# A sum over five columns moved from VectorE to additions on GpSimd, with columns outermost in the picture, and the next group's features placed between slices of the patch convolution

## The chip, the cores and the metric

The kernel runs on one NeuronCore of a Trainium2 chip. The metric is device time in microseconds (us) of one execution. Five engines work side by side, each on its own in-order queue, and meet only at semaphores: TensorE (PE: matmuls, PEld: its weight loads), VectorE (DVE), ScalarE (ACT), GpSimd (POOL) and SyncE (SP), which here only issues DMA transfers.

## The reference, cut to what matters

Four residual layers follow each other on 32 images of 32 channels and 32x32 pixels; `_gn` normalises every channel of every image:

```python
x = x + _L0_conv_ref(_gn(x), ...)   # 8x8 patches, each routed to 1 of 8 experts' 3x3 convolution
x = x + _L1_conv_ref(_gn(x), ...)   # one mixed 3x3 convolution per image
x = x + _L2_conv_ref(_gn(x), ...)   # nearest of 512 codes for each pixel
x = x + _L3_conv_ref(_gn(x), ...)   # deformable 3x3 convolution
```

The change touches two of them. The fourth samples each image, for every output pixel and each of 9 taps, at a fractional position:

```python
off = einsum('nchw,oc->nohw', inputs, w_grid) + b_grid
px, py = (base + koff + off + 1) * 0.5 * (W - 1)
sampled = tap(x0, y0, wx0*wy0) + tap(x1, y0, wx1*wy0) + tap(x0, y1, wx0*wy1) + tap(x1, y1, wx1*wy1)
out = conv(sampled, w_conv, strides=(3, 3))
```

The first takes a 10x10 window around each of 25 patches per image, routes by the window's mean (`feat = patched.mean(axis=(2, 3))`, the features) and convolves each patch with the chosen expert's weights.

## The kernel before, in words

The images go through in 8 groups of 4 (4 images x 32 channels fill the 128 partitions). A group g has a **front** (layers one to three, and the offsets of the fourth) and then 32 **tiles** (the sampling of the fourth layer; one tile is 128 output pixels of one image). The tiles of group g-1 are laid between the pieces of the front of group g. Every engine's program calls the same function `front(g)`, which calls `at(slots)` at fixed places: `ROW_SLOTS = {0: (-7, -6), 1: (-6, -4), 2: (-4, -3), 3: (-3, -1), 4: (-1, 0)}` after each of the five slices of the patch convolution, then `Y_SLOTS = (0, 3)`, `POOL_SLOTS = (3, 5)`, `MIX_SLOTS = (5, 7)`, `CONV1_SLOTS = (7, 9)`, `NORM2_SLOTS = (9, 11)`, seven `SCORE_SLOTS`, and so on to `REST_SLOTS`. The numbers count tiles from the group's first. So the order is written out by hand, and is the same on all engines. Behind the last front come 39 tiles with nothing between them (the tail): the last 7 of group 6 and the 32 of group 7.

**A tile** goes like this. SP fetches the tile's row positions, broadcast to all partitions, into one of `SPREADS = 4` buffers `zs` (L308). ACT makes tent weights from them, two activations L514 and one L517, into one of three buffers `tent`, two tiles ahead of PE. PE multiplies tents with the picture into three PSUM banks in turn, one bank for each third of the nine taps (L1014, 12 matmul records a third, 36 a tile): for each output pixel that is three taps x 32 channels x 5 neighbouring columns. DVE multiplies each third by the five column weights `near` (L708, 480 elements) and sums the five columns (L713, a reduction 480 -> 96) into `samp`. PE transposes the 288 sums (L1001), ACT copies them out (L504), and for every fourth tile PE convolves (L990).

PE's order within slot N is: third 0 of tile N, then the transposes L1001 of tile **N-1**, then thirds 1 and 2 of tile N. A third needs its bank read by DVE three thirds ago (`strip_read`).

```python
            def slot(N):
                strips(N, 0)
                if N > 0:
                    turn_samples(N - 1)
                strips(N, 1)
                strips(N, 2)
```

**SP** issues row N+SPREADS+1 of `zs` in slot N, after the wait that frees its buffer. In `NORM3_SLOTS` (slots 21 and 22) it does this for the last time before a long series: `load_slice(k, 1)` and `load_slice(k, 2)`, 12 window transfers (L369) and one of weights (L371) each, and `load_picture`, 16 transfers (L319). Only then does it go on with `zs`, and after slot 25 there is one more `load_slice`, after slot 27 another.

**Features.** DVE normalises the next group's input (L645 to L665), sums the windows (L738, L742) and scales (L746) in one piece after the fifth slice (`features`), before the tiles of `Y_SLOTS`. It copies the windows out (L751, five copies) in the piece that routes the next group and mixes the second layer's weights (after `POOL_SLOTS`). GpSimd only issues the gathers of the experts' weights (L476), 16 in all, and no arithmetic.

Names of stretches used below: the *features piece*, the *pooled piece* (adding the first layer's result, normalising, up to L836, for which PE waits), the *mix piece* (route, windows, mix, up to L785), the *scores* (L1115 on PE, L882 and L884 on DVE: 32 of each per group, one tile between each four).

## Time and profile before

| | |
|---|---|
| median of 3 runs | 2766.87 us (2762.34 to 2772.3) |
| the profiled execution | 2759.06 us |
| its span | 2757.2 us |
| PE busy | 2132.4 us (77%) |
| DVE busy | 1811.6 us (66%) |
| ACT busy | 1524.7 us (55%) |
| POOL busy | 24.7 us (1%) |
| mean granted TensorE clock | 0.911 |
| L708, DVE multiply | 503.6 us, 768 times |
| L713, DVE sum over the columns | 501.5 us, 768 times |

The span is from the first instruction to the last. The shares are averages over stretches with quite different limits: in the tail PE is never idle, within a front it stops for several us at a time. The granted clock is 1.0 at the higher of TensorE's two levels (2.4 GHz).

### The profile page before, as it was taken

How to read it: one execution, taken by the hardware profiler on the slowest of the kernel's cores; microseconds unless marked ns; L12 is line 12 of the kernel's file. 1: busy time of each engine (PE TensorE's matmuls, PEld its weight loads, DVE VectorE, ACT ScalarE, POOL GpSimd, SP SyncE). 2: the span in 40 equal slices, each digit the busy share in tenths (PEclk: the TensorE clock that was granted, in tenths of full speed). 3: DMA queues.
4: the chain of work that ended last, by engine and by line, in shares of the span. 5: the costliest groups of instructions: out<-in, count | busy, mean ns of one | idle time of the engine just before them, and what ended most of it. 6: DMA issues, size and time to landing. Idle time of an engine off the chain costs nothing.

```text
span 2757.2 us, 51316 instructions
## 1 busy us (share of the span) xinstructions
PE 2132.4 (77%) x20658; PEld 1792.4 (65%) x20658; DVE 1811.6 (66%) x3534; ACT 1524.7 (55%) x1803; POOL 24.7 (1%) x35
## 2 busy tenths in 40 slices
PE   0274488787886978878788778878788798887999
PEld 0223465687666966578666776568766696667998
DVE  3365458667686666866677665866758665776776
ACT  0021356466564655556565465646656465656987
POOL 1000000000000000000000000000000000000000
PEclk9686699899998989989999889989899899998999
DMA  6643533273351842436333453327434182113331
GB/s 171 126 132 72 141 106 120 76 161 113 100 147 43 202 123 78 125 92 181 103 105 104 111 155 106 116 79 161 119 98 148 44 199 92 52 48 90 108 116 56
DMA packets 290577, 311.50 MB, mean 113 GB/s; under 512 B 238148, under 2 KB 249092, under 8 KB 286116
## 3 DMA queue, kind: packets, MB, share of 16 engines
q1 hardware_dynamic: 285828, 273.74, 36.5%
q0 software_dynamic: 3360, 30.27, 4.1%
q10 hardware_dynamic: 1152, 4.19, 0.5%
q8 instruction: 165, 2.70, 0.4%
q14 instruction: 72, 0.59, 0.1%
HBM read 251.65 MB, written 56.48 MB: 112 GB/s over the span
## 4 chain that ended last, share of the span: by engine, by line
PE 53%; DVE 19%; DVEq 8%; SPq 7%; ACT 5%; DMA 4%; issue 4%; ACTq 0%; POOL 0%; POOLq 0%
PE bank L1014 37%; PE bank L1096 5%; SPq L369 4%; DVE code L884 4%; DVEq L883 4%; PE bank L1001 3%; DVE samp L713 3%; PE bank L1115 2%; SPq L319 2%; DVE strip L708 2%; PE bank L1074 1%; DVEq L712 1%; ACT diag L581 1%; PE bank L1132 1%; PE bank L1156 1%
## 5 line engine op out<-in xcount | busy, mean ns | idle before, releaser
L1014 PE MATMUL bank<-picture,tent 128*128 128x160 f32 x9216 | 1420.5, 313 | 79.1 <-DVE strip L708 52.2
L1014 PEld LDWEIGHTS bank<-picture,tent 128*128 128x128 f32 x9216 | 1351.5, 201 | 109.5 <-issue 83.2
L708 DVE TENSOR_TENSOR strip<-bank,near 128x480 f32<-128x480 f32 x768 | 503.6, 656 | 586.2 <-PE bank L1014 585.3
L514 ACT ACTIVATE tent<-zs,row_at_sb 128x1152 f32<-128x1152 f32 x512 | 614.5, 1249 | 50.5 <-DMA zs<-z_rows 50.3
L517 ACT ACTIVATE tent<-tent 128x2304 f32<-128x2304 f32 x256 | 543.8, 2124 | 18.8 <-issue 1.7
L713 DVE TENSOR_REDUCE samp<-strip 128x96 f32<-128x480 f32 x768 | 501.5, 653 | 72.4 <-issue 2.7
L504 ACT COPY samp_t<-bank 96x384 f32<-96x384 f32 x256 | 120.6, 471 | 461.9 <-PE bank L1001 461.8
L1115 PE MATMUL bank<-cb,xs 128*128 128x512 f32 x512 | 267.3, 624 | 118.6 <-DVE code L884 86.4
L1115 PEld LDWEIGHTS bank<-cb,xs 128*128 128x128 f32 x512 | 83.3, 191 | 259.4 <-issue 173.7
L574 ACT COPY xs<-xn 32x128 f32<-32x128 f32 x256 | 75.0, 293 | 195.6 <-PE bank L1115 177.8
L1001 PE MATMUL bank<-ident_sb,samp 128*96 128x128 f32 x768 | 138.5, 292 | 53.3 <-ACT fin L500 47.4
L882 DVE MAX8 top<-bank 128x8 f32<-128x512 f32 x256 | 174.7, 682 | 6.2 <-PE bank L1115 6.0
L884 DVE FIND_INDEX8 code<-top,bank 128x8 uint32<-128x512 f32 x256 | 176.8, 691 | 0.3 <-issue 0.3
L493 ACT ACTIVATE sd<-ve 128x1 f32<-128x1 f32 x32 | 6.5, 203 | 247.2 <-DVE ve L654 247.2
L1096 PE MATMUL bank<-xp,bd 128*128 128x512 f32 x288 | 130.9, 603 | 8.6 <-DVE bd L858 8.6
L1001 PEld LDWEIGHTS bank<-ident_sb,samp 128*96 128x96 f32 x768 | 87.8, 134 | 76.2 <-issue 53.9
L581 ACT ACTIVATE diag<-ident_h,code_f 128x128 f16<-128x128 f16 x256 | 81.8, 390 | 74.7 <-DVE code_f L908 74.7
L808 DVE TENSOR_TENSOR yc<-bank,gb 128x320 f32<-128x320 f32 x40 | 19.3, 483 | 124.3 <-PE bank L1074 124.3
L1096 PEld LDWEIGHTS bank<-xp,bd 128*128 128x128 f32 x288 | 53.4, 192 | 68.9 <-issue 60.3
L1074 PE MATMUL bank<-slice 96*32 96x64 f32 x1920 | 36.1, 242 | 71.0 <-DMA slice<-picked_weights 70.4
L1132 PEld LDWEIGHTS bank<-onehot,codes_b 128*32 128x32 bf16 x3072 | 48.5, 103 | 58.4 <-issue 33.1
L1074 PEld LDWEIGHTS bank<-slice 96*32 96x32 f32 x1920 | 34.3, 125 | 73.8 <-DMA slice<-picked_weights 72.9
(125 smaller groups left out, 1061.5 us busy)
## 6 DMA issues: line engine op xcount, KB each, us to landing
zs<-z_rows SPq DMA_DIRECT2D x256, 576.0 KB, 4.2
picked_weights<-arena SPq DMA_DIRECT2D x15, 1800.0 KB
arena<-picked_weights SPq DMA_DIRECT2D x24, 720.0 KB, 6.6
arena<-windows SPq DMA_DIRECT2D x288, 50.0 KB, 4.0
slice<-picked_weights SPq DMA_DIRECT2D x16, 720.0 KB, 6.1
windows<-arena SPq DMA_DIRECT2D x32, 312.5 KB, 5.0
slice<-windows SPq DMA_DIRECT2D x192, 50.0 KB, 2.9
y_patches<-yc SPq DMA_DIRECT2D x32, 160.0 KB, 4.4
```

The lines of the kernel that those rows point to most:

```text
L369: sp.dma_start(xs0[s][C * dy:C * (dy + 1), i], a[:, :, dy * WIN:dy * WIN + CUT]).then_inc(sliced[s], 16)
L504: act.copy(samp_t[:, N % SET], PT[0:PARTK, 0:384].rearrange("p (r n) -> p r n", r=3)).then_inc(samp_sb, 1)
L514: act.activation(w[:, c], zs[:, N % SPREADS, :], ACT.Abs, bias=row_at[:, c:c + 1])
L517: act.activation(w, w, ACT.Relu, bias=1.0, scale=-1.0).then_inc(tent_ready, 1)
L708: dve.tensor_tensor(y, STRIPS[j % 3][:, 0:DENSE * XW * C].rearrange("p (d c x) -> p d c x", d=DENSE, c=C), w.broadcast_to([128, DENSE, C, ...
L713: m = dve.tensor_reduce(samp[:, N % 2, PARTK * d:PARTK * (d + 1)], strip[:, j % 2], AX.X, ALU.add)
L882: dve.max(top[:, i, :], SCORES[n % 2][:, :])
L884: dve.max_index(code[:, i, :], top[:, i, :], SCORES[n % 2][:, :]).then_inc(score_read, 1)
L1001: m = pe.transpose(PT[0:PARTK, 128 * r:128 * (r + 1)], samp[:, N % 2, PARTK * r:PARTK * (r + 1)], ident[:])
L1014: m = pe.matmul(STRIPS[j % 3][:, XW * C * e:XW * C * (e + 1)], tent[:, N % TENTS, c, DENSE * d + e], picture[:, b % 2, i, c], start=(c == ...
L1096: m = pe.matmul(PP[1 + h][:, :], bd1[:, d, :], grid1[:, y:y + H // 2, d % 3:d % 3 + W], start=(d == 0), stop=(d == TAPS - 1))
L1115: pe.matmul(SCORES[n % 2][:, :], xs2[:, i, :], cb2[:], start=True, stop=True).then_inc(score_done, 1)
```

## The change

1. **The sum goes to GpSimd.** The picture is kept with columns outside channels (ACT's copy L525 now copies straight), so that the product strip is laid out tap, column, channel. DVE only multiplies. The reduction over five columns becomes three GpSimd additions per third: columns 0,1 += columns 2,3 (192 elements), column 0 += column 4 (96), samp = column 0 + column 1 (96), with a drain between them. PE's transposes wait for these (`added`). DVE may be three thirds ahead (`STRIPPED = 3`).
2. **SPREADS is 3** instead of 4.
3. **The next group's features** are split: normalising after slice 2, window sums after slice 3. The windows are copied out after the first tile of `Y_SLOTS`. SP sends the means out before the y transfers and fetches them after.
4. **Gathers.** Both halves of the picked weights have a place in the arena; GpSimd issues both gathers one after the other, between the additions of tiles 10 and 11 of a group. `q2` gets a buffer of its own.

```diff
-SPREADS = 4
+SPREADS = 3
+STRIPPED = 3
-                act.copy(picture[:, b % 2, i].rearrange("p k (c x) -> p k c x", c=C),
-                         raw[:, i].rearrange("p k (x c) -> p k c x", c=C)).then_inc(picture_ready, 1)
+                act.copy(picture[:, b % 2, i], raw[:, i]).then_inc(picture_ready, 1)
...
+            def tiles(first, end):
+                for N in range(max(first, 0), end):
+                    for d in range(THIRDS):
+                        j = THIRDS * N + d
+                        pool.wait_ge(strip_read, j + 1)
+                        if d == 0 and N >= 2:
+                            pool.wait_ge(samp_turned, N - 1)
+                        y = strip[:, j % STRIPPED]
+                        pool.tensor_tensor(y[:, :, 0:2], y[:, :, 0:2], y[:, :, 2:4], ALU.add)
+                        pool.drain()
+                        pool.tensor_tensor(y[:, :, 0], y[:, :, 0], y[:, :, 4], ALU.add)
+                        pool.drain()
+                        pool.tensor_tensor(samp[:, N % 2, PARTK * d:PARTK * (d + 1)].rearrange("p (d c) -> p d c", c=C),
+                                           y[:, :, 0], y[:, :, 1], ALU.add).then_inc(added, 1)
+
+            pick_weights(0)
+            for g in range(GROUPS):
+                base = GROUP_TILES * (g - 1)
+                tiles(base - 7, base + NORM2_SLOTS[1])
+                if g + 1 < GROUPS:
+                    pick_weights(g + 1)
+                tiles(base + NORM2_SLOTS[1], base + GROUP_TILES - 7)
+            tiles(ALL - GROUP_TILES - 7, ALL)
...
                     dve.wait_ge(strip_done, j + 1)
-                    y = strip[:, j % 2].rearrange("p (d c) x -> p d c x", d=DENSE)
-                    w = near[:, b % 2, i, t, DENSE * d:DENSE * (d + 1)].unsqueeze(2)
-                    dve.tensor_tensor(y, STRIPS[j % 3][:, 0:DENSE * XW * C].rearrange("p (d c x) -> p d c x", d=DENSE, c=C),
-                                      w.broadcast_to([128, DENSE, C, XW]), ALU.mult).then_inc(strip_read, 1)
-                    if d == 0 and N >= 2:
-                        dve.wait_ge(samp_turned, N - 1)
-                    dve.drain()
-                    m = dve.tensor_reduce(samp[:, N % 2, PARTK * d:PARTK * (d + 1)], strip[:, j % 2], AX.X, ALU.add)
-                m.then_inc(samp_ready, 1)
+                    if j >= STRIPPED:
+                        dve.wait_ge(added, j - STRIPPED + 1)
+                    w = near[:, b % 2, i, t, DENSE * d:DENSE * (d + 1)].unsqueeze(3)
+                    dve.tensor_tensor(strip[:, j % STRIPPED],
+                                      STRIPS[j % 3][:, 0:DENSE * XW * C].rearrange("p (d x c) -> p d x c", d=DENSE, c=C),
+                                      w.broadcast_to([128, DENSE, XW, C]), ALU.mult).then_inc(strip_read, 1)
...
                     at(ROW_SLOTS[v])
                     gate(v)
-                if k:
-                    features(k)
-                at(Y_SLOTS)
+                    if v == 2 and k:
+                        normalise(k)
+                    if v == 3 and k:
+                        features(k)
+                first, end = Y_SLOTS
+                at((first, first + 1))
+                if k:
+                    windows(k)
+                at((first + 1, end))
+                if k:
+                    copy_features(k)
...
-                pe.wait_ge(samp_ready, N + 1)
+                pe.wait_ge(added, THIRDS * (N + 1))
```

On GpSimd's queue, where before only the gathers stood (the place is the second half of its program, before):

```order
L476 DMA arena<-in_Wexp,expert 100x4608 [waits win_out3,sliced0,win_out2,sliced1,win_out1,sliced2,win_out0,expert_ready]
L476 DMA arena<-in_Wexp,expert 100x4608 [waits w_out,expert_ready]
L476 DMA arena<-in_Wexp,expert 100x4608 [waits win_out3,sliced0,win_out2,sliced1,win_out1,sliced2,win_out0,expert_ready]
L476 DMA arena<-in_Wexp,expert 100x4608 [waits w_out,expert_ready]
L476 DMA arena<-in_Wexp,expert 100x4608 [waits win_out3,sliced0,win_out2,sliced1,win_out1,sliced2,win_out0,expert_ready]
```

and around tile 11 of the first group now (strip is the product of one third, samp the sums):

```order
L498 TENSOR_TENSOR samp<-strip 128x96
L482 DMA arena<-in_Wexp,expert 100x4608 [waits sliced0,win_out3,sliced1,win_out2,sliced2,win_out1,picture_ready,win_out0,expert_ready]
L482 DMA arena<-in_Wexp,expert 100x4608
L494 TENSOR_TENSOR strip<-strip 128x3x64 [waits samp_turned,strip_read]
L496 TENSOR_TENSOR strip<-strip 128x3x32
L498 TENSOR_TENSOR samp<-strip 128x96
```

there are nine additions per tile in this queue, and the two gathers stand between those of two tiles.

On DVE's queue, after the fifth slice's gate (yc) in a middle group, before:

```order
L808 TENSOR_TENSOR yc<-bank,gb 128x320 [waits conv0_done]
L811 SCALAR_TENSOR_TENSOR yc<-yc,gb 128x320
L645 BN_STATS stats<-kept 128x6 [waits x_loaded3]
L645 BN_STATS stats<-kept 128x6
...
L665 TENSOR_SCALAR xp<-kept,mv,nr 128x32x32
L738 TENSOR_REDUCE rowsum<-xp 128x210
L742 TENSOR_REDUCE wsum<-rowsum 128x25
L746 TENSOR_SCALAR wsum<-wsum 128x25
L708 TENSOR_TENSOR strip<-bank,near 128x480 [waits strip_done]
```

and now, from slice 3's gate on:

```order
L832 TENSOR_TENSOR yc<-bank,gb 128x320 [waits conv0_done]
L835 SCALAR_TENSOR_TENSOR yc<-yc,gb 128x320
L762 TENSOR_REDUCE rowsum<-xp 128x210
L766 TENSOR_REDUCE wsum<-rowsum 128x25
L770 TENSOR_SCALAR wsum<-wsum 128x25
L735 TENSOR_TENSOR strip<-bank,near 128x480 [waits added,strip_done] x3
L832 TENSOR_TENSOR yc<-bank,gb 128x320 [waits conv0_done]
L835 SCALAR_TENSOR_TENSOR yc<-yc,gb 128x320
L735 TENSOR_TENSOR strip<-bank,near 128x480 [waits added,strip_done] x3
L775 COPY arena<-xp 128x500 x5
L735 TENSOR_TENSOR strip<-bank,near 128x480 [waits added,strip_done] x6
```

the normalising has gone one slice further up, a tile stands between each two pieces, and the window copies stand before the second tile of `Y_SLOTS`.

## Rows read from the trace of the kernel before

**Rows 1.** The page's part 4: the chain that ended last, by engine.
```profile
PE 53%; DVE 19%; DVEq 8%; SPq 7%; ACT 5%; DMA 4%; issue 4%; ACTq 0%; POOL 0%; POOLq 0%
```

**Rows 2.** The page's part 5: DVE's reduction (busy, mean ns, idle before).
```profile
L713 DVE TENSOR_REDUCE samp<-strip 128x96 f32<-128x480 f32 x768 | 501.5, 653 | 72.4 <-issue 2.7
```

**Rows 3.** Stretches' busy times: us, PE, PEld, DVE, ACT, POOL, PEclk, DMA, GB/s.
```profile
2560.00:2740.00 180.00, 179.69 (x1463) 173.78 (x1462) 128.51 (x197) 162.02 (x142) 0.00 (x0) 1.00 0.29 101
```

**Rows 4.** Timeline, slots 19 to 20 of a middle group: start, us, engine, line, [idle before].
```profile
1508.28 5.06 PE L1014 MATMUL bank<-picture,tent 128*128 128x160 f32 x36
...
1511.75 0.66 DVE L708 TENSOR_TENSOR strip<-bank,near 128x480 f32<-128x480 f32 x1 [0.23 <-PE bank L1014]
1512.50 0.65 DVE L713 TENSOR_REDUCE samp<-strip 128x96 f32<-128x480 f32 x1
1513.20 0.53 PE L1001 MATMUL bank<-ident_sb,samp 128*96 128x128 f32 x3
```

**Rows 5.** Groups by line and shape: small instructions of DVE, and of POOL.
```profile
L825 DVE TENSOR_TENSOR kept<-kept,arena 128x256 f32<-128x256 f32 x32 | 11.4, 418 | 1.7 <-DMA arena<-y_patches 1.7
L901 DVE TENSOR_TENSOR kept<-kept,arena 128x512 f32<-128x512 f32 x16 | 11.1, 692 | 1.2
L456 POOL DMA_DIRECT2D wroute<-in_w_route x4 | 2.1, 531 | 0.0
```

**Rows 6.** Timeline, the features piece of the same group.
```profile
1293.01 0.86 PE L990 MATMUL bank<-samp_t,wc 96*32 96x128 f32 x24
...
1298.06 3.54 PE L1014 MATMUL bank<-picture,tent 128*128 128x160 f32 x12 [4.19 <-DVE strip L708]
...
1301.82 5.25 PEld L1014 LDWEIGHTS bank<-picture,tent 128*128 128x128 f32 x36
```

**Rows 7.** Timeline, its mix piece.
```profile
1337.12 2.99 DVE L751 COPY arena<-xp 128x500 f32<-128x500 f32 x5
...
1337.66 0.19 ACT L564 ACTIVATE sm<-sm 128x4 f32<-128x4 f32 x1
...
1345.26 0.65 DVE L708 TENSOR_TENSOR strip<-bank,near 128x480 f32<-128x480 f32 x1
...
1346.05 2.78 PE L1014 MATMUL bank<-picture,tent 128*128 128x160 f32 x12 [4.14 <-DVE strip L708]
...
1349.32 0.88 PE L1001 MATMUL bank<-ident_sb,samp 128*96 128x128 f32 x3 [0.49 <-DVE samp L713]
```

**Rows 8.** Timeline, its scores: third, fourth and seventh rounds.
```profile
1420.21 1.99 PE L1115 MATMUL bank<-cb,xs 128*128 128x512 f32 x4
...
1421.38 0.70 DVE L882 MAX8 top<-bank 128x8 f32<-128x512 f32 x1 [0.42 <-PE bank L1115]
...
1432.70 1.88 PE L1115 MATMUL bank<-cb,xs 128*128 128x512 f32 x4
...
1434.22 0.69 DVE L882 MAX8 top<-bank 128x8 f32<-128x512 f32 x1
...
1469.54 1.98 PE L1115 MATMUL bank<-cb,xs 128*128 128x512 f32 x4
...
1472.12 0.69 DVE L882 MAX8 top<-bank 128x8 f32<-128x512 f32 x1
```

**Rows 9.** Timeline around the next group's boundary, SP and who waits.
```profile
1551.32 7.14 SPq L369 DMA_DIRECT2D arena<-windows  x12
...
1578.64 1.38 SPq L308 DMA_DIRECT2D zs<-z_rows  x3
...
1581.06 1.88 PE L1074 MATMUL bank<-arena 96*32 96x64 f32 x120
...
1582.94 2.40 ACT L514 ACTIVATE tent<-zs,row_at_sb 128x1152 f32<-128x1152 f32 x2 [9.85 <-DMA zs<-z_rows]
...
1587.58 3.57 PE L1014 MATMUL bank<-picture,tent 128*128 128x160 f32 x12 [4.64 <-ACT tent L517]
```

**Rows 10.** Waits of ACT for SP's row transfers: us, times, longest.
```profile
ACT tent L514 <- DMA zs<-z_rows: 50.3, 7, 10.1
```

More of the change, by code:

```diff
@@ L150, in build @@
         code_f = sb("code_f", [128, 2, IMG])
-        q2 = arena[:, SLICE + NV * ROWN:SLICE + NV * ROWN + PIX]
+        q2 = sb("q2", [128, PIX])
         xp3 = sb("xp3", [128, XP3])
@@ L158, in build @@
         tent = sb("tent", [128, TENTS, KC, TAPS, 128])
-        picked = [arena[0:ITEMS, 0:PICK],
-                  tent[:].rearrange("p u c d n -> p (u c d n)")[0:ITEMS, 0:PICK]]
+        picked = [arena[0:ITEMS, PICK * h:PICK * (h + 1)] for h in range(2)]
         picture = sb("picture", [128, 2, IMG, KC, XW * C])
-        strip = sb("strip", [128, 2, DENSE * C, XW])
+        strip = sb("strip", [128, STRIPPED, DENSE, XW, C])
         samp = sb("samp", [128, 2, TC])
@@ L246, in build @@
         strip_read = sem("strip_read")
+        added = sem("added")
         picture_ready = sem("picture_ready")
@@ L330, in tiles, with features_out, features_in @@
                         store(b, 0)
-            def features(k):
+            def features_out(k):
                 sp.wait_ge(wsum_ready, k + 1)
                 sp.dma_start(sum_dram.rearrange("i (c n) -> (i c) n", c=C), wsum[:]).then_inc(wsum_out, 16)
+            def features_in(k):
                 sp.wait_ge(wsum_out, 16 * (k + 1))
@@ L349, in store_weights @@
                 sp.wait_ge(w_picked[h], 16 * (k + 1))
-                sp.dma_start(w_dram[:, h, :], picked[h if k == 0 else 0]).then_inc(w_out, 16)
+                sp.dma_start(w_dram[:, h, :], picked[h]).then_inc(w_out, 16)
             def load_slice(k, v):
@@ L385, in front @@
                         load_slice(g, v + SLICES)
+                    if v == NV - 1 and k:
+                        features_out(k)
                 full = MOST * C // PATCHES
@@ L400, in front @@
                 if k:
-                    features(k)
+                    features_in(k)
                 at(Y_SLOTS)
-                at(POOL_SLOTS)
                 if k:
                     windows(k)
+                at(POOL_SLOTS)
                 at(MIX_SLOTS)
@@ L412, in front @@
                         store_weights(k, 0)
-                    if t == 5 and k:
+                    if t == 3 and k:
                         store_weights(k, 1)
@@ L429, in front @@
                     load_slice(k, 2)
+                    sp.wait_ge(w_out, 16 * 2 * (k + 1))
                 for i in range(IMG):
@@ L435, in front @@
                         spread_rows(N)
-            features(0)
+            features_out(0)
+            features_in(0)
             windows(0)
@@ L463, in _, with pick_weights @@
                 pool.dma_start(wc[:, r, :], A["w_conv"][PARTK * r:PARTK * (r + 1), :]).then_inc(loaded_later, 16)
-            def pick_weights(k, h):
+            def pick_weights(k):
                 pool.wait_ge(expert_ready, k + 1)
-                if k > 0 and h > 0:
-                    pool.wait_ge(w_out, 16 * (2 * k + 1))
-                if h == 0:
-                    for i in range(IMG):
-                        pool.wait_ge(win_out[i], 16 * (k + 1))
-                    if k > 0:
-                        pool.wait_ge(sliced[0], SLICED * 2 * k)
-                        pool.wait_ge(sliced[1], SLICED * 2 * k)
-                        pool.wait_ge(sliced[2], SLICED * k)
-                pool.indirect_dma_start(picked[h if k == 0 else 0], None, A["Wexp"],
-                                        bass.IndirectOffsetOnAxis(ap=expert[:, h:h + 1], axis=0)).then_inc(w_picked[h], 16)
@@ L479, in _ @@
-            for k in range(GROUPS):
-                for h in range(2):
-                    pick_weights(k, h)
+                for i in range(IMG):
+                    pool.wait_ge(win_out[i], 16 * (k + 1))
+                if k > 0:
+                    pool.wait_ge(sliced[0], SLICED * 2 * k)
+                    pool.wait_ge(sliced[1], SLICED * 2 * k)
+                    pool.wait_ge(sliced[2], SLICED * k)
+                if k > 1:
+                    pool.wait_ge(picture_ready, IMG * (k - 1))
@@ L730, in _, with normalise, features @@
             grid0 = xp0[:].rearrange("p (h w) -> p h w", w=G0)
-            def features(k):
+            def normalise(k):
                 dve.wait_ge(x_loaded[k % KEPT], 16 * (k // KEPT + 1))
                 norm(k, 0, x_of(k), grid0[:, 1:H + 1, 1:W + 1])
+            def features(k):
                 dve.drain()
@@ L817, in front @@
                     gate(v)
+                    if v == 2 and k:
+                        normalise(k)
[3 more added lines that the diff above has]
+                at((first, first + 1))
                 if k:
-                    features(k)
-                at(Y_SLOTS)
+                    windows(k)
+                at((first + 1, end))
+                if k:
+                    copy_features(k)
                 dve.wait_ge(y_in, 16 * 2 * IMG * (g + 1))
@@ L967, in front @@
                 at(REST_SLOTS)
+            normalise(0)
             features(0)
```

14 lines of the change are left out of this document (6 added, 8 removed).

## The prediction

> **What bounds the kernel now.** I read the chain of waits first: 53% of it is PE, 27% DVE and its queue, 7% SP's queue [rows 1]. So PE sets the pace, and DVE and SP only where PE stops for them. DVE's reduction costs 501.5 us busy [rows 2], but that isn't the gain: the question is where it stands between PE and its next matmul. Three kinds of stretch answer it.
>
> *Dense tiles*, in the tail above all: PE is busy 179.7 of 180 us, at full granted clock [rows 3]. Nothing can be gained there. PE's 36 matmul records of three thirds take 4.9 us from 1508.28 to the transposes at 1513.20, 1.63 us a third, and with 0.4 us for the transposes a tile is 5.3 us [rows 4]. The last third of a tile ends on PE one third before that, 1511.55; DVE multiplies from 1511.75 to 1512.41, reduces to 1513.15, and PE transposes at 1513.20 [rows 4]. The sum is just in time: from the end of the multiply to PE's transposes there are **0.79 us** and no more.
>
> *DVE pieces inside a front*: PE stops 4.19 us in the features piece and 4.14 us in the mix piece [rows 6, 7].
>
> *The group boundary*: SP issues slices and pictures from 1551.32 to 1578.64 and no row for a tile in between; ACT has then waited 9.85 us for a row, PE 4.64 us for its tent [rows 9]. There are seven such waits of ACT, 50.3 us together [rows 10].
>
> **What it gains.** Each per group, c being the time from the end of a multiply to the finished sum.
> - *Features piece.* PE's third 1 of the next tile starts at 1301.82; without the wait it would follow L990's end at 1293.87 after one third (1.63) and the transposes (0.4), at 1295.9 [rows 6, 4]. That is 6 us. In two pieces with tiles between, the wait is covered by three free banks, but GpSimd then has three thirds to catch up and PE's transposes wait for it: I take 1.5 us back. Gain 4.5, six groups: 27.
> - *Mix piece.* The five window copies (2.99 us) leave it, though DVE then waits for ACT's exponential, at 1337.66 [rows 7]; with one reduction less ahead it ends 2.8 us sooner, at 1342.5 instead of 1345.26. Three thirds then run through GpSimd until about 1347.7, where PE's transposes were at 1349.32 [rows 7]. Gain 1.7, six groups: 10. The moved copies stand in `Y_SLOTS`, where a tile leaves DVE over 3 us free; they cost nothing there. In group 0 nothing else is there: 3 more.
> - *Scores.* DVE's next unit starts at 1434.22, 1.52 us after PE's scores at 1432.70; where nothing held DVE it started 1.17 us after [rows 8]. Five rounds gain 0.35, the one with the residual 1.4 (2.58 less 1.17) [rows 8]. 3.1 a group, seven groups: 22. PE needs the rest of the round itself; most of the 2 us a round that DVE loses (three reductions) buys nothing.
> - *Pooled piece and three more places* where a DVE chain begins right behind a last third (one-hot, norm 3, z): a reduction's spacing, 0.7, each [rows 4], and 0.24 for a copy moved out: 3.1 x 7 = 21.
>
> Together **83 us**.
>
> **What it costs.**
> - *c.* The trace holds no arithmetic on GpSimd. Low end: as fast as DVE. 256 elements take 418 ns and 512 take 692 ns [rows 5], so 144 ns and 1.07 ns an element: three additions of 384 elements in all 0.84, with three handovers of about 0.09 (1512.41 to 1512.50 [rows 4]) 1.1 us. High end: three of 1.0 us, twice the smallest thing GpSimd does. That smallest takes 531 ns [rows 5], three of it 1.6 us. I take **1.6**, as GpSimd's own row is nearer than DVE's; ends 1.1 and 3.0. The Trainium skill, GPSIMD Engine Reference, Performance versus the Vector engine, gives a two-input fp32 addition about 2.6 cycles of 1.2 GHz an element (4497 ns for 2048); by it my estimate is 1.0 us for the three and 1.3 with handovers, and the whole sum would come out level. No row shows it.
> - *Dense tiles.* PE waits c - 0.79 = 0.8 us at the transposes. That counts wherever PE has nothing between the last third and the next tile's first: 48 places in the fronts (0 to 1 left out, where L990 covers; those in SP's hold too) and 29 of the tail's 38. 77 x 0.8 = **62 us**. Behind L990 (0.86 us), a convolution slice (1.88) or scores it is hidden. DVE's new wait for `added` has the next multiplies behind it and PE behind them through the banks; it costs nothing while three thirds on GpSimd take less than the tile, c up to about 2.
> - *SPREADS 3.* Slots 21 and 22 before fetched rows 26 and 27 ahead of SP's hold, now 25 and 26 (row N+4). Row 27 comes at 1578.64, where 28 came, and PE takes tile 27, not 28, at 1587.58. Tile 28 comes 5.3 us and a slice (1.88) later [rows 9]: 7.2 us a boundary. Such a hold is behind fronts 1 to 6 (slices are loaded for a next group): **43 us**. Elsewhere a row fetched 2 tiles ahead is in time.
> - Gathers, ACT's straight copy, means sent out before y: at nothing. The gathers delay tile 11's sums, which PE wants only behind four scores; what else they hide behind is gone only if GpSimd is late anyway (rival 3). SP's y transfers now wait for the window sums, DVE wants them only two tiles later, and SP's wait for the means' round trip is gone. ACT copies a picture in slots where it waits for SP or PE.
>
> Sum: -83 + 62 + 43 = +22 us on the profiled 2759.06 us, 2781. The median of the runs is 7.8 us above that execution: **2789 us**, 0.8% slower.
>
> A rule that speaks against the change: DVE's next chain starts while GpSimd is still adding. Nothing in this trace shows the two together. SBUF — State Buffer, of the Trainium skill, in its summary of the port pair, says that a VectorE instruction with two SBUF inputs (L825, L901) and a GpSimd one that reads SBUF exclude each other, the later waiting for the whole of the other. The multiply reads PSUM and one SBUF operand and would be free. By it I estimate 0.3 us at two chains a group, 4 us in all.
>
> **Rivals.**
> 1. *GpSimd is quick* (the other side: faster). Place: PE's transposes in the 77 dense places. With c = 1.1 they wait 0.3 us, 24 us in all, and the catching up gains 10: -93 + 24 + 43 = -26, 2741 us. It decides from c = 1.3 down, where costs and gains are even. For: 384 elements only. Against: three dependent instructions, each with a drain.
> 2. *The fourth buffer wasn't needed*: SP is slowed by the tiles' own pace, so rows come as before. Then -83 + 62 = -21, 2746 us. For: slower dense tiles use rows up later (two or three of them lie in the hold). Against: PE resumes at the same distance from SP's restart each time, and only the row's number changes.
> 3. *GpSimd is the bound.* With c over 2 three thirds take longer than PE's tile with its wait. At c = 2.2 dense tiles wait 1.4 us (108), and the gains in features and mix shrink by 20: +88, 2855 us. At c = 3.0 a tile takes 9 us and all is over 3000.
> 4. *The sum is hidden*: PE's queue takes the transposes late anyway. Then gain 83 - 43 = 40, 2727. Against: 1513.15 and 1513.20 [rows 4].
>
> **How the numbers follow.** Chances: forecast (c from 1.3 to 2.0, hold as worked out) 0.57; rival 1 0.17; rival 2 0.08; rival 3 0.14; rival 4 0.04. A difference under 0.3% (8 us) can't be told from none here. Rivals 1, 2 and 4 give most of faster, 0.27; the forecast's upper edge of speed, c near 1.3, gives same, 0.13; the rest slower, 0.60. The range takes rivals 1 and 2 and c up to 2.2: **2735 to 2857**; below lies rival 4, above c beyond 2.2. The forecast's own range, c from 1.3 to 2.0, is 2766 to 2830.
>
> **What the profile after would show.** Right: DVE about 500 us less busy; transposes in the tail released by GpSimd's last addition, a tile there 6.1 us and the tail's 39 tiles some 25 us longer; ACT's waits for rows 35 to 45 us longer than 50.3; PE's stops in the features and mix pieces under 2 us. Wrong: tail tiles at 5.3 us (then c is short, or the wait is covered), ACT's waits unchanged (rival 2), or DVE waiting for GpSimd in the tail (rival 3).

## The result, and the profile after

The changed kernel takes **2989.62 us** (median of 4 runs, 2985.87 to 2995.0) against 2765.52 us: a ratio of 1.081, 95% interval 1.0779 to 1.0838. Slower was right. The size was not: 224 us instead of 22, and 133 us above the upper end of the range.

The page of the changed kernel: engines, then the chain that ended last by engine and line, then the groups of the sum.

```profile
PE 2159.1 (72%) x20658; PEld 1805.8 (61%) x20658; DVE 1331.0 (45%) x2766; ACT 1518.2 (51%) x1803; POOL 1079.8 (36%) x2339
...
issue 59%; POOLq 27%; POOL 10%; DMA 3%; SPq 1%; DVE 1%; PE 0%; DVEq 0%; ACT 0%
...
L494 POOL TENSOR_TENSOR strip<-strip 128x192 f32<-128x192 f32 x768 | 461.7, 601 | 1369.9 <-DVE strip L735 1369.7
...
L496 POOL TENSOR_TENSOR strip<-strip 128x96 f32<-128x96 f32 x768 | 302.7, 394 | 280.5 <-issue 173.2
...
L498 POOL TENSOR_TENSOR samp<-strip 128x96 f32<-128x96 f32 x768 | 300.7, 392 | 113.5 <-issue 6.5
```

DVE's reduction [rows 2] is gone and DVE is busy 480.6 us less (1331.0 against 1811.6), and the kernel is slower: that time was hidden behind PE. The chain says little here: it follows GpSimd's queue, and 59% of it is time for which the profile shows no cause. The line to stop at is L496. It is the second of three additions on one engine and needs nothing but the first, yet its idle time before it is 280.5 us, of which 173.2 us have no releaser ("issue"). The waits of the same execution (us in total, times, longest) say how they are spread, and who pays:

```profile
PE bank L1030 <- POOL samp L498: 247.7, 98, 25.0
...
POOL strip L496 <- issue: 173.2, 13, 29.9
...
DVE strip L735 <- POOL samp L498: 113.3, 6, 20.4
ACT tent L541 <- DMA zs<-z_rows: 111.3, 15, 16.6
...
PE bank L1043 <- ACT tent L544: 55.2, 6, 11.2
```

L496 waited thirteen times, 29.9 us at the longest: six waits are of 25 to 30 us and hold 168.8 us, the other seven are trifles. The timeline shows where one stands (start, us, engine, line, idle before; middle of the program, GpSimd, DVE and PE):

```profile
1496.20 1.01 POOL L482 DMA_INDIRECT arena<-in_Wexp,expert  x1 [0.73 <-issue]
...
1497.52 1.00 POOL L482 DMA_INDIRECT arena<-in_Wexp,expert  x1 [0.30 <-issue]
...
1500.74 0.58 POOL L494 TENSOR_TENSOR strip<-strip 128x192 f32<-128x192 f32 x1 [2.22 <-DVE strip L735]
...
1529.48 0.39 POOL L496 TENSOR_TENSOR strip<-strip 128x96 f32<-128x96 f32 x1 [28.16 <-issue]
...
1530.49 0.66 DVE L735 TENSOR_TENSOR strip<-bank,near 128x480 f32<-128x480 f32 x1 [19.02 <-POOL samp L498]
...
1533.65 0.88 PE L1030 MATMUL bank<-ident_sb,samp 128*96 128x128 f32 x3 [23.29 <-POOL samp L498]
```

Between L494 and L496 there is only `pool.drain()` (L495). It is the first drain behind the two gathers of the expert weights, and it ends 28 us later. DVE has then stood 19.02 us without a free strip buffer, and PE 23.29 us without sums. The trace has the drains themselves too (ns: shortest, median, longest):

```profile
L495 POOLq DRAIN  x768: 671/677/30431, 313.6 to 2976.4; - x192
```

The same stands in each of the six fronts in which gathers are issued between tiles. The trace gives the time from a gather's issue to its landing; for the second gather of the first such pair (issued at 422.21) it is

```profile
DMA to landing us min/median/max: 31.7/31.7/31.7
```

so it landed at 453.9, and this is L496 there:

```profile
454.12 0.39 POOL L496 TENSOR_TENSOR strip<-strip 128x96 f32<-128x96 f32 x1 [28.10 <-issue]
```

This is 0.2 us after the landing. It is the same in the other five places: landings at 815.2, 1171.1, 1529.3, 1887.1 and 2246.0 us, L496 at 815.46, 1171.36, 1529.48, 1887.29 and 2246.21. From this came theory A: **a drain on GpSimd does not end before the data of the gathers issued ahead of it have landed.** Its rivals: the making of the gathers' descriptors keeps GpSimd or its port busy (B), PE has its work behind these waits anyway (C), and, later, that a drain behind a gather costs a fixed time (D).

The tail is the other thing to read (GpSimd, DVE, PE; a middle tile of it):

```profile
2917.38 0.66 DVE L735 TENSOR_TENSOR strip<-bank,near 128x480 f32<-128x480 f32 x1 [2.36 <-PE bank L1043]
2918.12 0.59 POOL L494 TENSOR_TENSOR strip<-strip 128x192 f32<-128x192 f32 x1 [1.37 <-DVE strip L735]
...
2919.01 0.66 DVE L735 TENSOR_TENSOR strip<-bank,near 128x480 f32<-128x480 f32 x1 [0.97 <-PE bank L1043]
...
2919.75 0.60 POOL L494 TENSOR_TENSOR strip<-strip 128x192 f32<-128x192 f32 x1
...
2921.02 0.39 POOL L498 TENSOR_TENSOR samp<-strip 128x96 f32<-128x96 f32 x1
...
2921.46 0.53 PE L1030 MATMUL bank<-ident_sb,samp 128*96 128x128 f32 x3 [0.85 <-POOL samp L498]
```

From the end of the multiply (2919.01 and 0.66 are 2919.67) to the end of the last addition (2921.41) are 1.74 us, where I took 1.6 for c; PE's transposes wait for it. A tile takes 6.28 us (the transposes of the tile before stood at 2915.18) instead of 5.3 [rows 4].

### The profile page after: what moved, and what is told of

Its sections match the earlier page's. It is cut to its first block, busy times and chain, and to the rows that moved or that the text cites. A ratio compares the mean times of both kernels' runs of the same rounds, so it can differ in the third digit from the quotient of the medians.

```text
span 2984.0 us, 54635 instructions
## 1 busy us (share of the span) xinstructions
PE 2159.1 (72%) x20658; PEld 1805.8 (61%) x20658; DVE 1331.0 (45%) x2766; ACT 1518.2 (51%) x1803; POOL 1079.8 (36%) x2339
## 3 DMA queue, kind: packets, MB, share of 16 engines
q10 hardware_dynamic: 1152, 4.19, 0.4%
## 4 chain that ended last, share of the span: by engine, by line
issue 59%; POOLq 27%; POOL 10%; DMA 3%; SPq 1%; DVE 1%; PE 0%; DVEq 0%; ACT 0%
POOLq L495 16%; POOLq L497 11%; POOL samp L498 10%; SPq L371 1%; DMA arena<-in_Wexp,expert 1%; DMA picked_weights<-arena 1%; POOL arena L482 0%; DMA y_patches<-yc 0%; DMA slice<-picked_weights 0%; DMA windows<-arena 0%; DMA window_means<-wsum 0%; DVE rowsum L762 0%; POOLq L492 0%; DMA kept<-in_x 0%; PE bank L1103 0%
## 5 line engine op out<-in xcount | busy, mean ns | idle before, releaser
L494 POOL TENSOR_TENSOR strip<-strip 128x192 f32<-128x192 f32 x768 | 461.7, 601 | 1369.9 <-DVE strip L735 1369.7
L496 POOL TENSOR_TENSOR strip<-strip 128x96 f32<-128x96 f32 x768 | 302.7, 394 | 280.5 <-issue 173.2
L1030 PE MATMUL bank<-ident_sb,samp 128*96 128x128 f32 x768 | 141.5, 297 | 295.6 <-POOL samp L498 247.7
L498 POOL TENSOR_TENSOR samp<-strip 128x96 f32<-128x96 f32 x768 | 300.7, 392 | 113.5 <-issue 6.5
L1030 PEld LDWEIGHTS bank<-ident_sb,samp 128*96 128x96 f32 x768 | 88.0, 135 | 329.8 <-POOL samp L498 272.7
```

Of the source, the lines that this page charges most:

```text
L494: pool.tensor_tensor(y[:, :, 0:2], y[:, :, 0:2], y[:, :, 2:4], ALU.add)
L496: pool.tensor_tensor(y[:, :, 0], y[:, :, 0], y[:, :, 4], ALU.add)
L498: pool.tensor_tensor(samp[:, N % 2, PARTK * d:PARTK * (d + 1)].rearrange("p (d c) -> p d c", c=C), y[:, :, 0], y[:, :, 1], ALU.add).then_i ...
L1030: m = pe.transpose(PT[0:PARTK, 128 * r:128 * (r + 1)], samp[:, N % 2, PARTK * r:PARTK * (r + 1)], ident[:])
```

## The experiments

Ten kernels ran, one of them twice. Each is compared with the kernel before on the same chip in the same stretch of time.

**1. own_sem.** The drains replaced by a semaphore between the same instructions.

```diff
-                        pool.tensor_tensor(y[:, :, 0:2], y[:, :, 0:2], y[:, :, 2:4], ALU.add)
-                        pool.drain()
-                        pool.tensor_tensor(y[:, :, 0], y[:, :, 0], y[:, :, 4], ALU.add)
-                        pool.drain()
+                        pool.tensor_tensor(y[:, :, 0:2], y[:, :, 0:2], y[:, :, 2:4], ALU.add).then_inc(halved, 1)
+                        pool.wait_ge(halved, 2 * j + 1)
+                        pool.tensor_tensor(y[:, :, 0], y[:, :, 0], y[:, :, 4], ALU.add).then_inc(halved, 1)
+                        pool.wait_ge(halved, 2 * j + 2)
```

> The changed kernel, with each of GpSimd's two drains per third replaced by a semaphore that the addition itself raises and the next one waits for. Theory A (the drain behind the two gathers of the expert weights doesn't end before the gathers' data has landed, 25 to 30 us in each of groups 1 to 6, 168.8 us in all): the six waits at the first of GpSimd's second additions vanish, the step from the last multiply to the sum stays near 1.7 us, 2990 - 150 = about 2840 us, and as low as 2810 if the throttled clock behind each wait goes too. Rival B (making the descriptors of the gathers keeps GpSimd's cores busy, or the port to SBUF is taken by them): the waits stay at 25 to 30 us, only the drains' own small cost changes, 2975 to 2995 us. Rival C (the waits are there but PE has its work behind them anyway): the waits vanish and the time moves by under 30 us.

Measured: **2813.31 us** (ratio 1.018, 1.0158 to 1.0202), 176 us less. GpSimd's timeline around two gathers:

```profile
1413.24 1.01 POOL L483 DMA_INDIRECT arena<-in_Wexp,expert  x1 [0.30 <-issue]
1416.61 0.58 POOL L495 TENSOR_TENSOR strip<-strip 128x192 f32<-128x192 f32 x1 [2.37 <-DVE strip L736]
1417.28 0.39 POOL L497 TENSOR_TENSOR strip<-strip 128x96 f32<-128x96 f32 x1
1417.74 0.39 POOL L499 TENSOR_TENSOR samp<-strip 128x96 f32<-128x96 f32 x1
```

This gather too lands 31.7 us after its issue, at 1444.9. All three thirds of tile 11 are summed by 1421.56, while it is under way, and none of their additions is longer than elsewhere. So making the descriptors doesn't keep GpSimd from adding (B falls), and PE needed the sums (C falls). PE's waits show most of the 176 us again:

```profile
PE bank L1031 <- POOL samp L499: 89.1, 92, 2.6
```

against 247.7 us: 158.6 less. About 18 us more are PE's busy time, 2159.1 against 2141.3 us. Behind the 23 us stop of the changed kernel, 24 matmuls took 4.69 us (1534.31, mean granted clock 0.73 from there to 1539), where they took 3.43 us ahead of it (1499.96, granted clock 1.00): this long stop cost a second time in the clock.

Not all of the 176 us are the six long waits. From one tile's transposes to the next, PE is 150.8 us slower than in own_sem in the two steps, to tiles 11 and 12, behind the six pairs of gathers. The other 20 to 25 us are spread over the program, 5.7 of them in the tail: there a drain only orders two additions, and c is 1.74 us with drains and 1.61 with semaphores.

**2. drain_probe.** The kernel before, where GpSimd does nothing but gather, with a marker on either side of a drain behind each gather.

```diff
+                pool.memset(probe[:, 0:1], 0.0)
+                pool.drain()
+                pool.memset(probe[:, 1:2], 0.0)
```

> The kernel before, where GpSimd has nothing but gathers to do, with three instructions behind each gather: a memset of one column, a drain, a memset of another column. Theory A (the drain waits until the gather's data has landed): the first memset follows the gather within 2 us, the second starts at the gather's landing, 13 to 25 us after its issue, within 0.5 us. Rival B (descriptor making keeps the cores busy): the first memset is late too. Rival D (a drain behind a gather costs some fixed time, whatever the landing): the second comes a constant time after the first. The kernel's time stays at 2766, or rises a little where the second gather of a group is held by the first one's landing, which its buffer makes it wait for anyway.

Measured: 2764.39 us, ratio 1.000 (0.9986 to 1.0019). GpSimd's timeline, three of the sixteen:

```profile
148.68 1.01 POOL L477 DMA_INDIRECT arena<-in_Wexp,expert  x1 [89.05 <-issue]
149.70 0.11 POOL L479 MEMSET probe<- 128x1 f32 x1
163.94 0.10 POOL L481 MEMSET probe<- 128x1 f32 x1 [14.12 <-issue]
176.83 1.01 POOL L477 DMA_INDIRECT arena<-in_Wexp,expert  x1 [12.79 <-DMA picked_weights<-arena]
177.85 0.12 POOL L479 MEMSET probe<- 128x1 f32 x1
191.81 0.10 POOL L481 MEMSET probe<- 128x1 f32 x1 [13.84 <-issue]
...
2095.56 1.01 POOL L477 DMA_INDIRECT arena<-in_Wexp,expert  x1 [68.86 <-DMA picked_weights<-arena]
2096.57 0.12 POOL L479 MEMSET probe<- 128x1 f32 x1
2114.30 0.10 POOL L481 MEMSET probe<- 128x1 f32 x1 [17.61 <-issue]
```

The three landed 15.1, 14.8 and 18.6 us after their issue, at 163.80, 191.67 and 2114.16. The first memset follows the gather at once; the second comes 0.14 us behind the landing each time, whether that is 14.8 or 18.6 us away. It is 0.14 or 0.15 us in fifteen of the sixteen, and 0.78 us behind the very first. A fixed cost (D) would not follow it, and descriptor making (B) would hold the first memset too. Theory A is shown, in a kernel without any addition on GpSimd. The Trainium skill, Perfetto Trace Analysis, DMA Instruction — SWDGE (GPSIMD), says that the profiler's end of such a DMA is the end of descriptor making and not that of the transfer; the trace agrees, 1.01 us against 14.8 to 18.6, and a reader who takes those 1.01 us for the gather's cost misses what the drain waits for.

**3. before_spreads3 and after_s4.** The third buffer of rows, alone in the kernel before and undone in the changed one.

```diff
-SPREADS = 4
+SPREADS = 3
```

> The kernel before with three row buffers instead of four and nothing else. By my term: 7.2 us at each of six boundaries, 2766 + 43 = 2809 us, PE's wait for its tent at the boundary about 12 us instead of 4.6. Rival (the fourth buffer isn't needed, my rival 2): within 8 us of 2766.

> The changed kernel with four row buffers again (SPREADS 4); two scratch tiles lie over a dead half of another one to make room. By my term for the third buffer: the rows of the tiles behind SP's hold come one tile earlier, ACT's waits for rows fall by 35 to 45 us of 111.3, 2990 - 43 = about 2947 us. Rival (the third buffer is enough because the tiles are slower and the gathers' wait sets the pace in each group): ACT's waits fall but the time stays within 10 us of 2990.

Measured: before_spreads3 **2808.41 us**, 45 more than before (ratio 1.0163, 1.0134 to 1.0192); after_s4 **2936.49 us**, 53 less than the changed kernel. The row of [rows 10], ACT's waits for rows, in before_spreads3 (PE's wait for tents there is 59.5 us, against 18.1 in the kernel before):

```profile
ACT tent L514 <- DMA zs<-z_rows: 113.1, 14, 16.6
```

My 43 us was right, and my rival 2 falls: PE's waits for tents grew by 41 us. ACT's waits for rows grew by 63 us, not by 35 to 45: ACT waits at more places than PE pays for.

**4. features_only.** The kernel before with the features' move alone (the hunks on `normalise`, `features`, `windows`, `copy_features`, `root` and `features_out` of the change; the diff is theirs).

> The kernel before with only the parts of the change that move DVE's work in the front: norm and window means between slices 2, 3 and 4 of the patch convolution, window copies and feature copy in the y slots, means sent out before y. By my terms, with no catching up through GpSimd: 6 us x 6 in the features piece, and in the mix piece the five window copies are gone but DVE waits for ACT's exponential, 1 to 2 us x 6; together about -42, 2724 us. Rival (PE's stop only moves to another place, where the tiles' banks run dry): 2755 to 2766 us.

Measured: **2722.21 us**, ratio 0.9836 (0.9809 to 0.9863), 41 less than before, and again 2723.52 (0.9866, 0.9851 to 0.9881), 37 less, when it ran beside experiment 8. The forecast of 42 for these moves holds as a sum, and this part alone beats both kernels. Its mix piece keeps a stop, of 2.01 us instead of 4.14 [rows 7]:

```profile
1327.63 1.87 PE L1025 MATMUL bank<-picture,tent 128*128 128x160 f32 x12 [2.01 <-DVE strip L713]
```

The parts of the sum are another matter. In PE's waits (us in total, times, longest; first the kernel before, then features_only):

```profile
PE bank L1040 <- DVE feat_t L757: 56.5, 8, 8.8
PE bank L1085 <- DVE sm L836: 9.2, 2, 9.0
```
```profile
PE bank L1096 <- DVE sm L848: 55.1, 8, 9.0
PE bank L1051 <- DVE feat_t L763: 13.2, 8, 2.2
```

PE's largest stop here before was neither of the two that my prediction names (4.19 and 4.14 us), but one of up to 8.8 us for the means of the next group. It went down to 2.2 us, and nearly as much came back at PE's next step, where it waits for the pooled piece (sm).

**5. own_sem_s4.** Experiment 1 with four row buffers.

> The changed kernel with both repairs: a semaphore between GpSimd's additions in place of the drains, and four row buffers. If the two costs are independent: 2813 - 50 = about 2763 us, level with before, that is, what the sum on GpSimd costs (its dense tiles) and what it gains beside features_only (2722) come to +41. Rival (the gathers' wait and the rows' hold overlapped in the changed kernel, so each repair already took part of the other): 2775 to 2790 us.

Measured: **2764.97 us**, ratio 1.0001 (0.9989 to 1.0013). The two repairs add up: 176 and 48. What is left between this kernel and features_only, 43 us, is the price of summing on GpSimd, together with what goes with it in the code (the layout, ACT's straight copy, the place of the gathers). It can be split by place, from the start times of PE's transposes, 256 in each trace. The stretch "11 to 18" is the time from the transposes that PE does in slot 11 to those in slot 18, added over the tiles of groups 1 to 6, and so on. Each column is one execution, up to 7 us away from its kernel's median; features_only's is 31 us shorter than before's, where the medians are 41 apart.

| stretch | before | features_only | own_sem_s4 | changed kernel | scores_on_pool |
|---|---|---|---|---|---|
| tiles -7 to 0 (slices) | 308.3 | 317.8 | 318.3 | 367.5 | 314.5 |
| 0 to 5 (y, pooled) | 284.5 | 254.5 | 261.4 | 268.1 | 252.4 |
| 5 to 7 (mix) | 124.9 | 111.5 | 126.6 | 129.8 | 111.7 |
| 7 to 11 | 272.7 | 273.7 | 277.9 | 277.9 | 274.7 |
| 11 to 18 (scores) | 552.8 | 556.6 | 530.4 | 654.9 | 528.9 |
| 18 to 25 | 410.9 | 409.8 | 422.9 | 424.5 | 410.5 |
| group 0, to tile 24 | 262.5 | 263.0 | 263.4 | 288.8 | 257.2 |
| tail, 38 tiles | 210.2 | 210.2 | 235.0 | 240.7 | 210.2 |

GpSimd's sums pay in one place only, between the scores: 26.2 us less than in features_only. They cost 24.8 us in the tail, 15.1 in the mix piece, 13.1 behind the scores and 11.1 in the stretches 0 to 5 and 7 to 11. The changed kernel's 124.5 us above own_sem_s4 in the score stretch are the gathers' waits of five fronts, and 117 of them stand in the one step to tile 11; the sixth is the 25 us in group 0.

**6. sum_on_dve.** The changed kernel with DVE reducing over the new layout.

```diff
-                        pool.tensor_tensor(y[:, :, 0:2], y[:, :, 0:2], y[:, :, 2:4], ALU.add)
...
+                    dve.tensor_reduce(samp[:, N % 2, PARTK * d:PARTK * (d + 1)].rearrange("p (d c) -> p d c", c=C),
+                                      strip[:, j % STRIPPED].rearrange("p d x c -> p d c x"), AX.X, ALU.add).then_inc(added, 1)
```

> The changed kernel with everything kept (columns outermost, third buffer of rows, features between slices, straight copy, gathers back to back) but the sum done by DVE in one reduction over the new layout; GpSimd only gathers. If the sum's place is the whole rest: 2722 (features alone) + 45 (third buffer alone) = about 2767 us, 46 below own_sem's 2813. In the tail a tile takes 5.3 us again instead of 6.28. Rival (the new layout costs or gains by itself: a reduction that reads its five columns 48 elements apart is slower, or ACT's straight copy, 457 ns against 754, gains): over 10 us away from 2767; a reduction of more than the 653 ns of before would show it.

Measured: **2893.41 us** (ratio 1.0467, 1.0436 to 1.0498), 126 over the 2767. The rival was right, and here is its number (busy, mean ns):

```profile
L728 DVE TENSOR_REDUCE samp<-strip 128x96 f32<-128x480 f32 x768 | 772.1, 1005 | 72.2 <-issue 2.3
```

1005 ns against 653 [rows 2], for the same 480 elements. The five columns of a sum now lie 32 elements (128 bytes) apart, not 48 as I had written, instead of side by side. The columns-outermost layout suits additions of whole columns, and not this reduction. The Trainium skill, SBUF — State Buffer, in its section on the DMA port swizzle, says that accesses which leave a 16-byte line pay a penalty; the reduction agrees, and no run here tells that apart from another cause in DVE. This run is no measure of the sum's place, therefore; experiment 5 is.

**7. hybrid_s4.** own_sem_s4 with a tile's last third summed on DVE, the first two on GpSimd.

```diff
-                    for d in range(THIRDS):
+                    for d in range(THIRDS - 1):
...
+                dve.tensor_reduce(samp[:, N % 2, PARTK * d:PARTK * (d + 1)].rearrange("p (d c) -> p d c", c=C),
+                                  strip[:, d].rearrange("p d x c -> p d c x"), AX.X, ALU.add).then_inc(samp_ready, 1)
```

> own_sem_s4 with the sums of a tile's first two thirds on GpSimd and of the last one on DVE. The dense tiles lose their wait (the last third is reduced as in before, 5.3 us a tile in the tail), while DVE keeps two reductions in three less. If my dense term is right (77 tiles by 0.97 us is 75) and the scores gain 0.35 us a round by the missing reductions: below features_only's 2722, 2690 to 2710 us. Rival (DVE's time behind the scores is hidden anyway, or GpSimd and DVE slow each other at the port: the multiply took 681 ns alone and 726 beside GpSimd in places): 2722 to 2740 us.

Measured: **2773.99 us** (ratio 1.0041, 1.0024 to 1.0058), outside both the forecast and its rival: a miss. The reduction takes 1013 ns in this layout too; the forecast counted on the 653 ns of before. Counted as in the table above, the hybrid's tail is shorter than own_sem_s4's (220.1 us against 235.0) and its score stretch longer (567.2 against 530.4, and against 556.6 in features_only). The 681 and 726 ns of the rival are not the multiply's, which takes 656 and 657 ns, but those of the addition to `fin` (L719 before, L742 in the changed kernel).

**8. scores_on_pool.** The sum on GpSimd only in tiles 11 to 17 of a group, in the layout of before; all else as in features_only.

```diff
+        def on_pool(N):
+            return N < GROUP_TILES * (GROUPS - 1) and 11 <= N % GROUP_TILES < 18
...
                 for N in range(max(first, 0), end):
+                    if not on_pool(N):
+                        continue
                     for d in range(THIRDS):
...
+                    if on_pool(N):
+                        continue
                     dve.drain()
                     m = dve.tensor_reduce(samp[:, N % 2, PARTK * d:PARTK * (d + 1)],
                                           strip[:, d].rearrange("p d c x -> p (d c) x"), AX.X, ALU.add)
```

> A version put together from what the runs so far showed: features_only's order of DVE's work, four row buffers, the sum on DVE everywhere except in the seven tiles of a group that stand between the scores, where GpSimd adds all three thirds with a semaphore of its own, in the layout of before (columns innermost, ACT reorders the picture), so that DVE's reductions stay at 653 ns. From the transposes' times, the score stretch (tiles 11 to 17, six groups) took 556.6 us in features_only and 530.4 in own_sem_s4, 26 less, while every other stretch was shorter or as short in features_only. If stretches add up: 2722 - 26 - 4 (group 0) = about 2692 us, below features_only and before. Rival (GpSimd's additions with a stride of five elements are slower than the 600 and 390 ns of contiguous rows, as DVE's reduction over the other layout was, 1005 ns against 653): the stretch gains less, 2700 to 2730 us.

> features_only once more, to stand beside scores_on_pool on the same chip: 2722 us, 0.984 of before.

Measured: **2696.97 us** (5 runs, 2690.11 to 2705.16), ratio 0.9783 (0.9768 to 0.9798): the fastest of all, 26.6 us below features_only beside it, and 5 over the forecast. In the table's two executions it is 38 us below, 27.7 of them in the score stretch and 5.8 in group 0; the 5.4 in the first two stretches are not explained. GpSimd's three groups:

```profile
L503 POOL TENSOR_TENSOR strip<-strip 128x192 f32<-128x192 f32 x147 | 78.0, 530 | 927.7 <-DVE strip L745 925.1
L505 POOL TENSOR_TENSOR strip<-strip 128x96 f32<-128x96 f32 x147 | 68.3, 465 | 11.5
L507 POOL TENSOR_TENSOR samp<-strip 128x96 f32<-128x96 f32 x147 | 58.8, 400 | 11.5
```

Elements 20 bytes apart cost GpSimd 465 and 400 ns where contiguous ones cost 394 and 392; the first addition, with pairs of neighbours, is even shorter (530 against 601). The three come to 1395 ns against 1387, so the new layout was not needed for GpSimd either.

**9. fourth_add.** own_sem with one more addition of 96 elements ahead of each third's three.

```diff
+                        pool.tensor_tensor(out, y[:, :, 0], y[:, :, 1], ALU.add).then_inc(halved, 1)
+                        pool.wait_ge(halved, 3 * j + 1)
```

> own_sem with a fourth, needless addition of 96 elements in each third, ahead of the other three (about 0.47 us with its semaphore): the sum is there 0.47 us later. If PE's wait in the dense tiles is what the sum on GpSimd costs: the tail's 38 tiles take 0.47 us more each (18 us), the 48 dense places of the fronts as much (23 us), 2813 + 41 = about 2854 us, and 2845 to 2870 with what the catching up loses. Rival (GpSimd's three thirds, now about 6.2 us of a 6.2 us tile, become the bound): the tail takes over 0.8 us more a tile, and the time is over 2880. Rival (PE's wait in the tail has another cause, the multiplies' wait for added): under 5 us more in the tail.

Measured: **2919.53 us** (ratio 1.0573, 1.0557 to 1.0589), 106 more than own_sem for one addition of 0.39 us a third. The tail's 38 tiles take 265.5 us instead of own_sem's 235.0, 0.80 more each. GpSimd and PE in its tail:

```profile
2868.81 0.39 POOL L496 TENSOR_TENSOR samp<-strip 128x96 f32<-128x96 f32 x1 [0.69 <-DVE strip L738]
...
2870.76 0.39 POOL L496 TENSOR_TENSOR samp<-strip 128x96 f32<-128x96 f32 x1
...
2872.80 0.54 PE L1033 MATMUL bank<-ident_sb,samp 128*96 128x128 f32 x3 [1.50 <-POOL samp L502]
```

A third now holds GpSimd for 1.95 us (2868.81 to 2870.76), longer than PE's 1.63 [rows 4]. So the last third, for which the transposes wait, is begun 0.32 us late and lasts 0.46 us longer than in own_sem (the addition and its semaphore): PE waits 1.50 us where it waited 0.72. From the second third's first addition at 2868.81 to the transposes are 3.99 us. The first rival is right in its size (0.80 us a tile, over 2880 us), though GpSimd isn't busy without a break (0.69 us idle ahead of the first row): what decides is its pace in a third, not in a tile.

## Why the prediction was wrong

The step that failed is in the last item of the costs: **"Gathers, ACT's straight copy, means sent out before y: at nothing. The gathers delay tile 11's sums, which PE wants only behind four scores"**. It gave the gathers no time at all, and c had the drains only as handovers of about 0.09 us. The wait was made by the two together: a drain behind a DMA that takes 29 to 33 us to land. Experiment 1 puts drains at 176 us of the 224, about 150 of them at the six pairs of gathers. No rival held it: rival 3 made GpSimd late by the pace of its arithmetic, and 2855 us was its mildest form.

Could the trace of before have shown it? Not the drain's rule; GpSimd had no drain there. But the gathers' time from issue to landing, 13.8 to 24.8 us there, stood in it, and the change put nine additions and six drains for each tile behind them on the same queue. A bound from above was due for that place, as it was given for c: six times a landing, 150 us.

The other terms, by the forecast's own parts:

| term | forecast | measured | by |
|---|---|---|---|
| features and mix piece | -40 (27 + 10 + 3) | -41 (-37 the second time) | features_only less before |
| sum on GpSimd | +19 (62 - 22 - 21) | +43 | own_sem_s4 less features_only |
| SPREADS 3 | +43 | +48 (+45 alone, +53 in the changed kernel) | own_sem less own_sem_s4 |
| drains and gathers | 0 | +176 | changed kernel less own_sem |
| together | +22 | +226 | beside experiments 1 to 4, where before took 2763.34 us |

- *Features and mix piece.* That -40 meets -41 is in part luck. The 27 had 1.5 us a group taken off for GpSimd's catching up and the 10 a reduction gone, and features_only has neither; and the stop that it takes away is mostly the one of 8.8 us that the prediction doesn't name, with a new one in its place (experiment 4). By the table the stretch 0 to 5 gains 30.0 us and the mix piece 13.4, the slices lose 9.5, and group 0, for which I had 3, gains nothing.
- *c.* I took 1.6 us from GpSimd's smallest row [rows 5] between ends of 1.1 and 3.0. It is 1.74 us with drains and 1.61 with a semaphore (2745.00 to 2746.61 in own_sem's tail). The row was the right neighbour. By my estimate from the Trainium skill's GPSIMD Engine Reference, Performance versus the Vector engine, 1.3 us, the sum would have come out level; the trace doesn't agree with the estimate. 192 elements take 601 ns and 96 take 394. That is 2.16 ns an element, which agrees with the page's 2.6 cycles of 1.2 GHz, and 187 ns that each of these additions costs besides. The page's 2.6 cycles give 0.83 us for 384 elements; my 1.0 us left 0.17 for the three such parts, which measured 0.56.
- *Dense tiles.* Right in place: in the tail a tile goes from 5.29 to 6.27 us, and one with L990 in it stays at 6.25 to 6.28, as said. A tile grows by 0.98 us where I took 0.8 (0.86 in own_sem, whose tile is 6.15): 30.5 us in the tail against 23.
- *Scores.* 26 us in six groups against a forecast of 19 (22 in seven): right in kind, a little small.
- *Sum on GpSimd.* The missing 24 us stand mostly where I had called GpSimd's catching up free: in the mix piece (15.1 us above features_only; I had reckoned a gain) and behind the scores (13.1). There DVE hands over several thirds at once, and GpSimd takes 1.60 us for each in the changed kernel (1530.35 to 1531.95) and 1.49 in own_sem_s4, not much less than PE's 1.63. My reading, which no run tests by itself, is that it doesn't catch up before PE wants the sums. And my "costs nothing while three thirds on GpSimd take less than the tile, c up to about 2" fails: in experiment 9 three thirds take 5.85 us of a tile of 6.93, and it costs 106 us. The limit lies below 1.95 us a third; PE's 1.63 would fit.
- *Places where a DVE chain begins behind a third.* They came, smaller: PE's stop in norm 3 went from 7.29 to 6.58 us, z from 6.27 to 5.68, one-hot from 3.14 to 2.91.
- *DVE beside GpSimd.* The rule that spoke against the change, with 4 us, came about. The additions that read two SBUF operands in the y stretch (L825 before, L857 in the changed kernel) take 530 ns in the mean instead of 418: 14 of the 32 take 403 to 412 ns and 18 take 602 to 809. Each of the 18 meets an addition of GpSimd, and ten of the 14 short ones meet none; with the other four, which follow each other in the first front, GpSimd is the one that is held, one L494 taking 1.87 us instead of 0.60. On DVE's side that is 3.6 us.
- *SPREADS 3.* Right in place and size (forecast 7.2 us a boundary, 45 / 6 = 7.5).
- *The sign* was right, with a chance of 0.60, but for reasons that make less than a quarter of the loss: without the drains the changed kernel is at 2813 us, inside the range, 24 us above the forecast.

## What to carry to other kernels

Before arithmetic is put on an engine's queue that also issues DMAs, ask of each fence in it what else it waits for. On GpSimd, order two dependent instructions with a semaphore of their own, and use no drain within a landing's time behind a gather. Work moved off a busy engine pays only in the stretches where that engine is waited for: take each stretch's gain apart (here 26 us in seven tiles of 32) and move the work only there. And where a helper's pace per unit falls behind the path's, a delay counts more than once (here 0.46 us a third became 0.80 us a tile).

## What the runs showed of the hardware that I had not expected

- A drain on GpSimd doesn't end before the indirect DMAs issued ahead of it have landed: the instruction behind it starts 0.22 us behind the landing in all six places of the changed kernel, and 0.14 or 0.15 us in fifteen of the sixteen of drain_probe. GpSimd's other instructions run beside the transfer. Whether other kinds of DMA on GpSimd, or drains on other engines, behave so was not tried.
- Two gathers issued back to back (1.3 us apart) land after 19 to 26 and 29 to 33 us in the changed kernel's six fronts; alone, in drain_probe, after 14.6 to 18.6.
- DVE's reduction of 480 elements to 96 takes 653 ns with the five addends side by side and 1005 ns with them 128 bytes apart.
- GpSimd's additions cost 187 ns and 2.16 ns an element (from 601 ns for 192 and 394 for 96), and up to 18% more at 96 elements with a step of 20 bytes (465 against 394 ns).
- DVE's additions of two SBUF operands took 602 to 809 ns instead of 403 to 412 where they met an addition of GpSimd, in 18 of 22 such meetings; in the other four, one behind another, GpSimd's addition took 1.87 us instead of 0.60.
